# One matmul per batch for a group's shared values in two attention layers, and self attention in rows of (head of the pair, query) in the fp8 layer

## The reference, cut to what matters

```python
def _gqa(q, k, v):
    scale = 1.0 / np.sqrt(q.shape[-1])
    scores = jnp.einsum('bsghd,btgd->bghst', q, k) * scale
    p = jax.nn.softmax(scores, axis=-1)
    return jnp.einsum('bghst,btgd->bsghd', p, v)
...
core = _gqa(q, k, v).reshape(b, s, nh * d)
...
xout = _gqa(qx, kx, vx).reshape(b, s, nh * d)
cat = jnp.concatenate([core, xout], axis=-1)
catq = _div_clamp_fp8(cat, proj_smooth)
```

## Time and profile before

| | |
|---|---|
| median of 3 runs | 4199.12 us (4195.64 to 4205.3) |
| profiled execution | span 4201.9 us, its own time; nothing else is recorded of it |
| third cross-attention layer, first to last matmul row | 2071.9 to 2428.9 us |
| fp8 layer, first to last matmul row | 2794.7 to 3519.3 us |

### The profile page before, as it was taken

One profiled execution on the slowest core, in us unless ns is written; L12 is line 12 of the kernel. 1 busy time (PEld: TensorE's weight loads), 2 busy tenths in 40 slices (PEclk: granted clock), 3 DMA queues, 4 the chain that ended last, 5 costly groups with the idle time before them and its releaser, 6 DMA issues. The chain is left out here.

```text
span 4201.9 us, 69897 instructions
## 1 busy us (share of the span) xinstructions
PE 3507.0 (83%) x26670; PEld 2513.1 (60%) x26672; DVE 2632.8 (63%) x5424; ACT 1714.6 (41%) x3298; POOL 357.1 (8%) x570
## 2 busy tenths in 40 slices
PE   7999998998876888874499876979899996887878
PEld 4556656887764655653266633535566665766767
DVE  6888896444266777788665563237887775444552
ACT  4888895111144343433243312225545451323222
POOL 3000000000000000000011100011112111111000
PEclk8555556999887666665799888989999997998787
DMA  2000001000001000001000014000000003000000
GB/s 82 1 0 0 0 0 75 0 0 20 1 18 48 2 2 2 2 2 62 6 5 7 6 62 141 0 3 3 2 5 2 2 3 122 1 1 1 1 1 11
DMA packets 44880, 73.71 MB, mean 18 GB/s; under 512 B 25805, under 2 KB 33490, under 8 KB 41046
## 3 DMA queue, kind: packets, MB, share of 16 engines
q1 hardware_dynamic: 36440, 70.54, 4.8%
q10 hardware_dynamic: 8256, 0.52, 0.2%
HBM read 67.91 MB, written 3.15 MB: 17 GB/s over the span
## 5 line engine op out<-in xcount | busy, mean ns | idle before, releaser
L1316 DVE TENSOR_SCALAR_CACHE_REDUCE l0x_ex<-l0x_s_ps 128x1024 f32<-128x1024 f32 x258 | 305.6, 1222 | 63.5 <-PE l0x_s_ps L1019 62.5
L1151 ACT ACTIVATE l0x_ex<-l0x_ex,l0x_neg_max,l0x_q_scale 128x2048 f32<-128x2048 f32 x128 | 268.0, 2094 | 52.4 <-DVE l0x_neg_max L1322 50.6
L1031 PEld LDWEIGHTS l0x_t_ps<-l0x_identb,l0x_pb 128*128 128x128 bf16 x2048 | 200.2, 143 | 109.3 <-issue 57.6
L1019 PE MATMUL l0x_s_ps<-l0x_kT,l0x_qT 64*128 64x512 bf16 x516 | 235.4, 600 | 32.8 <-ACT l0x_qT L1146 19.5
L1158 ACT ACTIVATE l0x_pt<-l0x_t_ps 128x1024 bf16<-128x1024 bf16 x256 | 246.2, 1013 | 32.4 <-PE l0x_t_ps L1031 32.4
L1031 PE MATMUL l0x_t_ps<-l0x_identb,l0x_pb 128*128 128x128 bf16 x2048 | 233.9, 305 | 6.7 <-ACT l0x_pt L1158 4.1
L1331 DVE TENSOR_SCALAR l0x_pb<-l0x_ex 128x2048 bf16<-128x2048 f32 x128 | 156.3, 1222 | 0.0
L263 PE MATMUL l3x_bank<-l3x_w_kv_x,l3x_ctxT 128*128 128x512 f32 x256 | 121.7, 619 | 18.1 <-ACT l3x_ctx_q L762 10.7
L263 PE MATMUL l3x_bank<-l3x_wproj,l3x_cat 128*128 128x256 f32 x512 | 119.5, 387 | 15.5 <-DVE l3x_cat L3367 15.5
L1019 PEld LDWEIGHTS l0x_s_ps<-l0x_kT,l0x_qT 64*128 64x128 bf16 x516 | 50.0, 121 | 129.0 <-issue 80.8
L2118 PEld LDWEIGHTS l1a_bank<-l1a_u,l1a_gm 64*64 64x64 f32 x2048 | 113.1, 221 | 9.5 <-issue 8.5
(11 more groups left out here) (741 smaller groups left out, 8452.7 us busy)
## 6 DMA issues: line engine op xcount, KB each, us to landing
l3x_wproj<-in_L_xattn_wproj SPq DMA_DIRECT2D x1, 4096.0 KB, 24.1
l3a_w<-in_L_attn_W SPq DMA_DIRECT2D x4, 1024.0 KB, 11.6
l2f_w<-in_L_ffn_w SPq DMA_DIRECT2D x1, 2816.0 KB, 11.3
l0x_ctxT<-in_ctxT SPq DMA_DIRECT2D x8, 256.0 KB, 2.8
l0a_wq<-in_L_attn_W_Q SPq DMA_DIRECT2D x1, 2048.0 KB
l0a_wk<-in_L_attn_W_K SPq DMA_DIRECT2D x1, 2048.0 KB
l0a_wv<-in_L_attn_W_V SPq DMA_DIRECT2D x1, 2048.0 KB, 8.1
l0a_wo<-in_L_attn_W_O SPq DMA_DIRECT2D x1, 2048.0 KB, 13.2
```

What stands on the lines that cost most here:

```text
L1019: ins = mm(s_ps[:, j * 512:(j + 1) * 512], qT[rows, h // 2, :], kT[rows, h // 2, j * 512:(j + 1) * 512], start=True, stop=True)
L1031: ins = nc.tensor.transpose(t_ps[:, j * P:(j + 1) * P], pb[:, h % 2, j * P:(j + 1) * P], identb[:])
L1151: s.activation(ex[:, h % 4, :], ex[:, h % 4, :], ACT.Exp, scale=q_scale[:, h:h + 1], bias=nb[:, h:h + 1], accum_out=sums[:, h:h + 1]).then ...
L1316: v.tensor_scalar(ex[:, h % 4, c], s_ps[:, c], 1.0, None, ALU.mult, ALU.max, accum_out=mx[:, h, half:half + 1]).then_inc(o.up(scores_taken ...
```

## The change

First, `WideAttention` gets `shared`, the number of heads that share values (4 in the third cross-attention layer, 2 in `cross` of the fp8 layer). `mix` then does one matmul for these heads and a batch: the same weights (the values), and as moving data the columns of all the heads, in runs of 64 with 64 others between; the output goes to the bank in the same runs. A half of 8 heads has 4 matmuls with 256 columns in the third cross-attention layer, and 8 with 128 in the fp8 layer, where both had 16 with 64.

Second, the self attention of the fp8 layer becomes a class of its own, `PairAttention`. The partitions of its scores are (head of the pair, query) where they were (batch, query), and (pair, batch, key) lie along the free side. So the weights have no zeros: `pb` and its clearing are gone, `weigh` is one instruction over 128 partitions, and all 16 heads are turned by 8 transposes at once, copied by ScalarE bank by bank. The mix has one matmul per pair and batch, with the 64 partitions of that batch's keys as contraction, 128 columns, and the output in the bank of the batch. The out copies write runs of 64.

The diff, cut:

```diff
--- before.py
+++ after.py
@@ -788,8 +788,8 @@
 
     HEADS = 16
 
-    def __init__(self, L, name, keys, scale, s_bank, t_bank, q, k, v, e, pb, pt, oT, mask=None, o_bias=None, o_factor=None, primed=False):
-        self.L, self.keys, self.scale, self.s_bank, self.t_bank = L, keys, scale, s_bank, t_bank
+    def __init__(self, L, name, keys, scale, s_bank, t_bank, q, k, v, e, pb, pt, oT, mask=None, o_bias=None, o_factor=None, primed=False, shared=1):
+        self.L, self.keys, self.scale, self.s_bank, self.t_bank, self.shared = L, keys, scale, s_bank, t_bank, shared
         self.q, self.k, self.v, self.mask, self.o_bias, self.o_factor = q, k, v, mask, o_bias, o_factor
         self.groups = 1 if keys == S else 2
         self.gh, self.per = self.HEADS // self.groups, 512 // keys
@@ -825,13 +825,15 @@
         pe.wait_ge(self.pT_ready.sem, self.pT_ready.value(t, half + 1))
         if half:
             pe.wait_ge(self.out_taken.sem, self.out_taken.value(t, half))
-        for h in range(8):
-            out = self.s_bank[h // 4][:, (h % 4) * P:(h % 4 + 1) * P]
+        n = self.shared
+        for h in range(0, 8, n):
             if self.keys == S:
-                ins = self.L.nc.tensor.matmul(out, self.v(half * 8 + h, 0), self.pt[:, h, :], start=True, stop=True)
+                ins = self.L.nc.tensor.matmul(self.s_bank[h // 4][:, (h % 4) * P:(h % 4 + 1) * P], self.v(half * 8 + h, 0), self.pt[:, h, :], start=True, stop=True)
             else:
+                out = self.s_bank[h // 4][:].rearrange("p (h q) -> p h q", q=P)[:, h % 4:h % 4 + n, :]
                 for b in range(2):
-                    ins = self.L.nc.tensor.matmul(out[:, b * S:(b + 1) * S], self.v(half * 8 + h, b), self.pt[:, h, b * S:(b + 1) * S], start=True, stop=True)
+                    q = slice(b * S, (b + 1) * S)
+                    ins = self.L.nc.tensor.matmul(out[:, :, q], self.v(half * 8 + h, b), self.pt[:, h:h + n, q], start=True, stop=True)
         ins.then_inc(self.out_ps.sem, 1)
 
     def exponential(self, o, g):
@@ -883,6 +885,90 @@
             ps = self.s_bank[j][:].rearrange("p (h q) -> p h q", q=P)
             by, op = (self.o_factor, ALU.mult) if self.o_factor is not None else (self.o_bias, ALU.add)
             v.tensor_tensor(self.oT[:, h:h + 4, :], ps, by[:, h:h + 4].unsqueeze(2).broadcast_to([P, 4, P]), op).then_inc(o.up(self.out_taken if j else None), 1)
+
+
+class PairAttention:
+    HEADS, PAIRS = 16, 8
+
+    def __init__(self, L, name, scale, s_bank, t_bank, q, k, v, e, pt, oT, o_factor):
+        self.L, self.scale, self.s_bank, self.t_bank = L, scale, s_bank, t_bank
+        self.q, self.k, self.v, self.o_factor = q, k, v, o_factor
+        self.e, self.pt, self.oT = e, pt, oT
...
+    def score(self, pe, t):
+        for pair in range(self.PAIRS):
+            for b in range(2):
+                u = (pair % 4) * 2 + b
+                for n in range(2):
+                    out = self.s_bank[pair // 4][n * S:(n + 1) * S, u * S:(u + 1) * S]
+                    ins = self.L.nc.tensor.matmul(out, self.q(2 * pair + n, b), self.k(2 * pair, b), start=True, stop=True)
+        ins.then_inc(self.scores_ps.sem, 1)
+
+    def turn(self, pe, t):
+        pe.wait_ge(self.probs.sem, self.probs.value(t))
+        for j in range(2):
+            for i in range(4):
+                u = 2 * (4 * j + i)
+                ins = self.L.nc.tensor.transpose(self.t_bank[j][:, i * P:(i + 1) * P], self.e[:, u:u + 2, :].rearrange("p u k -> p (u k)"), self.L.env.ident[:])
+            ins.then_inc(self.pT_ps.sem, 1)
+
+    def mix(self, pe, t, half):
+        pe.wait_ge(self.pT_ready.sem, self.pT_ready.value(t, half + 1))
+        if half:
+            pe.wait_ge(self.out_taken.sem, self.out_taken.value(t, half))
+        for i in range(4):
+            pair = 4 * half + i
+            for b in range(2):
+                r = slice(b * S, (b + 1) * S)
+                ins = self.L.nc.tensor.matmul(self.s_bank[b][:, i * P:(i + 1) * P], self.v(pair)[r, :], self.pt[r, pair, :], start=True, stop=True)
+        ins.then_inc(self.out_ps.sem, 1)
+
+    def exponential(self, o):
+        o.eng.wait_ge(self.shifted.sem, self.shifted.value(o.t))
+        e = flat(self.e)
+        self.L.nc.scalar.activation(e, e, ACT.Exp, scale=self.scale).then_inc(o.up(self.exped), 1)
+
+    def take_turned(self, o):
+        for j in range(2):
+            o.eng.wait_ge(self.pT_ps.sem, self.pT_ps.value(o.t, j + 1))
+            self.L.nc.scalar.activation(flat(self.pt[:, 4 * j:4 * j + 4, :]), self.t_bank[j][:], ACT.Copy).then_inc(o.up(self.pT_ready), 1)
+
+    def shift(self, o):
+        v = self.L.nc.vector
+        o.eng.wait_ge(self.scores_ps.sem, self.scores_ps.value(o.t))
+        for j in range(2):
+            e, mx = self.e[:, 8 * j:8 * j + 8, :], self.mx[:, 8 * j:8 * j + 8]
+            ps = self.s_bank[j][:].rearrange("p (u k) -> p u k", k=S)
+            v.reduce_max(mx, ps, AX_X).then_inc(o.up(), 1)
+            o.eng.wait_ge(o.sem, o.at())
+            v.tensor_tensor(e, ps, mx.unsqueeze(2).broadcast_to([P, 8, S]), ALU.subtract).then_inc(o.up(self.shifted if j else None), 1)
+
+    def weigh(self, o):
+        v = self.L.nc.vector
+        o.eng.wait_ge(self.exped.sem, self.exped.value(o.t))
+        v.reduce_sum(self.sum[:], self.e, AX_X).then_inc(o.up(), 1)
+        o.eng.wait_ge(o.sem, o.at())
+        v.reciprocal(self.inv[:], self.sum[:]).then_inc(o.up(), 1)
+        o.eng.wait_ge(o.sem, o.at())
+        v.tensor_tensor(self.e, self.e, self.inv[:].unsqueeze(2).broadcast_to([P, self.HEADS, S]), ALU.mult).then_inc(o.up(self.probs), 1)
+
+    def take_out(self, o, half):
+        v = self.L.nc.vector
+        o.eng.wait_ge(self.out_ps.sem, self.out_ps.value(o.t, half + 1))
+        h = slice(8 * half, 8 * half + 8)
+        by = self.o_factor[:, h].unsqueeze(2).broadcast_to([P, 8, S])
+        for b in range(2):
+            ps = self.s_bank[b][:].rearrange("p (h q) -> p h q", q=S)
+            v.tensor_tensor(self.oT[:, h, b * S:(b + 1) * S], ps, by, ALU.mult).then_inc(o.up(self.out_taken if b else None), 1)
 
 
 def l0_xattn_weights(W):
@@ -2727,7 +2813,7 @@
         att = WideAttention(L, "att", SC, float(P) ** -0.5, s_bank, t_bank,
                             q=lambda h, b: qT[:, h, b * S:(b + 1) * S], k=lambda h, b: kT[:, b, h // 4, :],
                             v=lambda h, b: vv[:, b, (h // 4) * P:(h // 4 + 1) * P], e=e, pb=pb, pt=pt, oT=oT,
-                            mask=lambda g, j: mask[:].unsqueeze(1).broadcast_to([P, 4, SC]), o_bias=bv, primed=True)
+                            mask=lambda g, j: mask[:].unsqueeze(1).broadcast_to([P, 4, SC]), o_bias=bv, primed=True, shared=H // KV)
         y_ps, tile_done = L.sig("y_ps"), L.sig("tile_done", primed=True)
         block = L.block()
 
@@ -3400,7 +3486,7 @@
         ctx_q, ctx_k, ctx_v = L.sb("ctx_q", [P, H, P]), L.sb("ctx_k", [P, 2, G, P]), L.sb("ctx_v", [P, 2, G * P])
         rows_ = [L.sb(f"rows{n}", [P, 8, P]) for n in range(2)]
         e = L.sb("e", [P, 2, 8, SC])
-        pb, pt = L.sb("pb", [P, H, P]), L.sb("pt", [P, 8, P])
+        pt = L.sb("pt", [P, 8, P])
         cat = L.sb("cat", [P, H, P])
         bank = L.banks(8)
         s_bank, t_bank, pair = bank[0:2], bank[2:4], (bank[4:6], bank[6:8])
@@ -3429,14 +3515,14 @@
         sk = heads("sk", 0, [fill(1, wk, i) for i in range(2)], [fours(own_k, i) for i in range(2)], "kln", own_scale["k"])
         sq0, sq1 = (heads(f"sq{n}", 1 - n, [fill(0, wq, 2 * n + i) for i in range(2)], [fours(own_q, 2 * n + i) for i in range(2)], "qln", own_scale["q"]) for n in range(2))
         sv = PlainPhase(L, "sv", pair[1], [fill(2, wv, i) for i in range(2)], [own_v[:, i * 512:(i + 1) * 512] for i in range(2)], scale=v_scale[:])
-        own = WideAttention(L, "self", S, float(P) ** -0.5, s_bank, t_bank,
+        own = PairAttention(L, "self", float(P) ** -0.5, s_bank, t_bank,
                             q=lambda h, b: own_q[:, h, b * S:(b + 1) * S], k=lambda h, b: own_k[:, h // 2, b * S:(b + 1) * S],
-                            v=lambda h, b: own_v[:, (h // 2) * P:(h // 2 + 1) * P],
-                            e=e[:, 0, :, :].rearrange("p h k -> p (h k)").rearrange("p (a h k) -> p a h k", a=1, k=S), pb=pb, pt=pt, oT=cat, o_factor=smooth_inv[:, 0:H])
+                            v=lambda pair: own_v[:, pair * P:(pair + 1) * P],
+                            e=e[:, 0, :, :].rearrange("p h k -> p (h k)").rearrange("p (u k) -> p u k", k=S), pt=pt, oT=cat, o_factor=smooth_inv[:, 0:H])
         cross = WideAttention(L, "cross", SC, float(P) ** -0.5, s_bank, t_bank,
                               q=lambda h, b: ctx_q[:, h, b * S:(b + 1) * S], k=lambda h, b: ctx_k[:, b, h // 2, :],
                               v=lambda h, b: ctx_v[:, b, (h // 2) * P:(h // 2 + 1) * P],
-                              e=e, pb=e[:].rearrange("p g h k -> p (g h) k"), pt=pt, oT=cat, o_factor=smooth_inv[:, H:2 * H], primed=True)
```

(8 more changed lines are left out.)

15 lines of the change are left out of this document (10 added, 5 removed).

## The result

| | changed | before |
|---|---|---|
| median (range, runs) | 4138.64 us (4136.65 to 4143.53, 4) | 4197.55 us (4195.64 to 4205.3, 4) |
| ratio, 95% interval | 0.9857 [0.9843, 0.9871] | 1 |
| span of the profiled execution | 4137.5 us | 4201.9 us |

A forecast was written before the change was run, and what follows sets the result against it. TensorE's own work bounds l2x; in the fp8 layer about a tenth of the tile is TensorE waiting. 28.1 + 31.9 - 15 = 45 us off 4201.9 gives 4156.9, as median 4154 us; range 4136 to 4174.

The forecast's parts named there:

- l2x, 28.1 us forecast: Third cross-attention layer: wide value matmuls save 3.03 us a tile, 21.2 over seven, plus 6.9 in the last tile.
- half 1 and the projection there stay at the lower clock: Last tile of l2x: clock at its lower level, both halves on the chain, 6.9 us saved.
- Cross in the fp8 layer: Wide value matmuls save 1.84 us in each half; half 0's turns into waits, half 1's passes.
- Self attention, 1.22 us a tile: Fp8 layer: VectorE's single weigh instruction brings 1.22 us a tile; the shorter self mix brings nothing.
- Layer's head and last tile: Fp8 layer: clearing of pb gone from the head, 1.8 us; last tile 8.7 us.
- The clock, 15 us: Steady fp8 tiles: falls to 1.2 GHz cost 2.1 us a tile, 15 over seven; bounds 0 and 32 us.
- the first place: Fp8 tile's stretch around the second self mix, between two fills: clock falls in nearly every tile, 1.7 to 2.9 us each.
- the second: Fp8 tile's thin stretch before the cross mix of half 1: a clock fall in one of five tiles.
- signs of being wrong: Records of 256 columns taking 0.4 or more, a steady l3x tile keeping clock 1.00, or a period above 85.3.
- The reading of the first tile: First fp8 tile: TensorE busy 4.03 us of 2865 to 2870 at full clock, then the clock fell.
- Rival (1): Whole kernel: the clock holds, 60.0 us gained, 4139 us; chance 0.17.
- The rule of the Trainium skill that was weighed: TensorE's clock drops only after long idle between bursts; by it nothing falls and the sum is the first rival's.

The follow-up runs named there:

- e1: Kernel before the change plus only the wide value matmuls in l2x: 4167.25 us, ratio 0.9927 to before.
- e4: Changed kernel with half 0 of the fp8 layer's cross mix narrow again (64 columns a matmul): 4141.61 us, ratio 0.9859 to before.
- e2: Kernel before the change plus only the wide value matmuls in the fp8 layer's cross attention: 4186.27 us, ratio 0.9969 to before.
- e4b: Changed kernel with half 1 of the fp8 layer's cross mix narrow again (64 columns a matmul): 4160.58 us, ratio 0.9918 to before.
- e11: Kernel before plus only the self attention in pairs, with 16 spare transposes around the second self mix: 4190.45 us, ratio 0.9973 to before.
- e7: Changed kernel with the self mix's row halves in turn, all of half 0 and then half 1: 4134.26 us, ratio 0.9848 to before.
- first profile: First profiled execution of the changed kernel, nothing else altered: span 4137.5 us, median of its runs 4138.64 us.
- e3: Kernel before the change plus only the self attention in pairs: 4196.54 us, ratio 0.999 to before.
- e6: Changed kernel with 16 spare transposes, 8 ahead of and 8 behind the second self mix: 4136.85 us, ratio 0.9851 to before.
- e10: Changed kernel with cross half 1 ahead of the next query turn, 16 spare transposes and self-mix row halves in turn: 4129.41 us, ratio 0.9816 to before.
- second profile: Profile of the changed kernel run once more, nothing altered: 4134.77 us, ratio 0.9851 to before.

## Why the prediction was right in its range and 15 to 19 us too slow

- **l2x, 28.1 us forecast, 32.6 measured.** Each tile gave 2.96 against 3.03; the record of 256 columns (0.23 us) and the wait of 0.38 at the query turn came nearly as worked out. The last tile was mis-sized: 6.9 forecast, 44.8 - 32.9 = 11.9 measured. What failed is the premise that half 1 and the projection there stay at the lower clock. e1 repeats it.
- **Cross in the fp8 layer.** Half 0 is hidden (e4: 0.1 us a tile), half 1 passes whole (e2: 85.30 - 83.49 = 1.81; e4b: its mix 1.7 longer with the same wait behind it). Both steps right; the waits for ScalarE (0.48, 0.39) stand where they were put.
- **Self attention, 1.22 us a tile.** Right, with 1.35 measured, but seen alone only in e11: 85.3 to 83.95. That the mix's own length is worth nothing in a steady tile is shown by e7. A steady tile of the whole was forecast at 82.2 without the clock and takes 82.1.
- **Layer's head and last tile.** 1.8 forecast; VectorE's first reciprocal comes 1.99 us after the last write of `x_stream` where it came 4.24 after it, 2.3 less, and the whole head up to the first self score is 2.4 shorter. The last tile gave 84.5 - 74.4 = 10.1 against 8.7, again because the second cross mix found full clock (2.05).
- **The clock, 15 us.** This is the step whose reasoning failed. The place is right, and a fall costs what I said: 2.1 and 2.4 us in the first profile, and at the lower end 1.4 in e3 and 1.7 in e2, within 1.7 to 2.9 but for e3. More work there goes with fewer falls, not with none (one left in e6, two in e11, none in e10). What was wrong is "a fall in nearly every tile at the first place and in one of five at the second": at the first place four of seven in one execution and two of seven in the other. The seven periods were to give 21.4 - 15 = 6.4 us; they gave 596.6 - 585.8 = 10.8 in the first profile and 596.6 - 578.1 = 18.5 in the second. So the term is 10.6 and 2.9 us, not 15. Two of the signs of being wrong that the prediction named came up: three steady tiles kept clock 1.00, and one period was above 85.3.
- **How often it falls.** The mistake was to judge the place from the work in it. The reading of the first tile was off by some 2 us too: the granted clock fell there at 2871.9 us, and the 5 us right ahead of it had 3.17 busy, not the 4.03 of the earlier trace rows; the steady stretch with 3.17, which kept its clock, lies at a later place of its tile, and at the same place (3122.1 to 3127.1) TensorE was busy 3.66 there. And e2 falls with the old self attention, e3 and e4b in every tile, the changed kernel between, while before and e1 fall only in the first tile. What fixes the moment in which a tile falls is left open. What the runs show is that, once a tile of e2, e3 or e4b fell, every later one did, and the falls came 85.3 us apart, although e2's tiles without a fall take 83.49.

By terms for the first profile: l2x 32.6, fp8 layer 23.4, stages that nothing changed 9.8 - 1.0 - 0.4, together the 64.4 of the span. The two layers gave 56.0 in the first profile and 64.3 in the second, where 45 was forecast with the clock and 60 without.

So the 19.4 us between the forecast span (4156.9) and the first profile's are: 8.4 from stages that nothing changed, 5.0 from l2x's last tile, 4.4 from the seven fp8 periods (the clock's term above all), 2.1 from the fp8 layer's head and last tile, less 0.5 in l2x's steady tiles. Only in the second profile is the clock the largest part (12.1). Rival (1), the clock holds, gave 4139 and 4138.64 was measured, but that is luck: the clock didn't hold in four of seven tiles, and the mis-sized last tiles and the stages that nothing changed made up for it.

The rule of the Trainium skill that was weighed (TensorE: Matmul & The Clock Gate, Why this matters for your kernels: the clock drops after long idle gaps) would have given the better number and for the wrong reason: at the first place the clock fell behind waits of 0.9 to 1.1 us at most, in four periods of the first profile and in each of e3. The rule of the Trainium skill (PSUM — Partial Sum Buffer, Specifications (TRN2)) that any access that isn't contiguous slows matmuls significantly does not hold here for runs of 64 columns: 8 records of 256 columns take 1.73 and 1.85 us, where unbroken ones would take 1.78.

## What to carry to other kernels

Cost a shortened step by what waits next behind it: of four halves made 1.7 to 1.8 us shorter, one passed nothing, one seven tenths and two all of it. Where a stage runs with TensorE near the point at which its clock falls, price one fall from rows and let the count go from none to every tile, and compare versions by the length of the stage and of its tiles, not by the kernel's time. A gain there may need idle TensorE time filled with spare work before it is seen: e11's tiles show it for 1.35 us, e10's for 0.9, each in one profile.

## What was not expected of the hardware

- Tiles with the same instructions have the clock fall or not (e2: 83.49 and 85.18 us), and in e2 from the fourth tile on, in e3 and in e4b falls came at even distances of 85.3 us in every tile.
- TensorE was busy 3.28 of the 5 us ahead of a fall to 1.2 GHz in one tile of e2, and 3.29 at the same place of the tile before, which held 2.4 GHz; in the changed kernel 3.12 and 3.12.
- Matmuls with 64 rows on different halves of the array overlap partly: 16 records in 1.16 us against 1.71 in turn.
- In l2x's last tile the clock came back earlier with the shorter mixes: half 0 went from 7.09 to 3.78 us at the lower clock, and half 1 behind it from 7.09 to 1.99 at the full one, 5.1 us where the lower clock would have left some 3.3. All ten profiles with the wide mixes have this last tile at 32.8 to 32.9 us, all four without at 44.8 to 44.9; why it comes back earlier is not shown.
